# Value products of two key tiles in one block of eight half units, over a ring of sixteen exponential buffers

## The reference

```python
def _expert(x, Wqkv, bqkv, Wo, bo, g1, be1, W1, bf1, W2, bf2, g2, be2):
    q, k, v = jnp.split(x @ Wqkv.T + bqkv, 3, axis=-1)      # each to 8 heads of 16
    attn = jax.nn.softmax(jnp.einsum('bhqd,bhkd->bhqk', q * scale, k), axis=-1)
    ctx = jnp.einsum('bhqk,bhkd->bhqd', attn, v)            # heads joined again
    x = _layernorm(x + ctx @ Wo.T + bo, g1, be1)
    h = jax.nn.gelu(x @ W1.T + bf1, approximate=False)
    h = jax.nn.gelu(h @ W2.T + bf2, approximate=False)
    return _layernorm(x + h, g2, be2)
```

## Time and profile before

| what | us |
|---|---|
| median of the runs | 5361.68 |
| profiled execution, its own time | 5363.5 |
| its span | 5361.7 |
| TensorE busy | 4544.8 (85%) |
| ScalarE busy | 2978.1 (56%) |
| VectorE busy | 2919.5 (54%) |
| granted TensorE clock, mean share | 0.907 |

### The profile page before, as it was taken

The page is one execution under the profiler, slowest core; times in us unless marked ns, Lnnn a source line. Parts: engine busy times, 40 slices in busy tenths (PEclk is TensorE's granted clock), DMA queues, the critical chain, the costliest instruction groups (busy, mean ns, idle before and its releaser), DMA issues.

```text
span 5361.7 us, 86367 instructions
## 1 busy us (share of the span) xinstructions
PE 4544.8 (85%) x25404; PEld 2517.8 (47%) x25404; DVE 2919.5 (54%) x6875; ACT 2978.1 (56%) x6402; POOL 706.2 (13%) x477
## 2 busy tenths in 40 slices
PE   4599997888659999788866999978885699997888
PEld 3344443466434444356643444435663344443566
DVE  5577772234457777224445777722444577762244
ACT  1177775643218777564322877755441287775543
POOL 0212221000022222100001222200000122220000
PEclk8699998999769999899966999989996799998999
DMA  2133320000123332000013323100001333220000
GB/s 90 19 46 46 53 33 15 14 21 18 50 28 44 46 46 33 15 16 18 20 48 36 44 40 50 26 15 20 16 20 46 38 46 44 43 40 1 24 12 23
DMA packets 97883, 174.96 MB, mean 33 GB/s; under 512 B 18848, under 2 KB 75600, under 8 KB 96720
## 3 DMA queue, kind: packets, MB, share of 16 engines
q1 hardware_dynamic: 97488, 170.00, 18.2%
HBM read 94.13 MB, written 1.53 MB: 18 GB/s over the span
## 4 chain that ended last, share of the span: by engine, by line
issue 50%; PE 42%; DVE 3%; POOL 1%; POOLq 1%; DMA 1%; DVEq 1%; ACT 1%; SPq 0%; ACTq 0%
PE ps L767 10%; PE ps L803 10%; PE ps L777 9%; PE ps L837 3%; PE ps L846 3%; PE ps L758 2%; PE ps L864 2%; DVE peaks L1520 1%; POOL rstd L526 1%; DMA k_stack<-parts 1%; PE ps L632 1%; PE ps L827 1%; PE ps L869 1%; DVE xn L1364 1%; PE ps L786 0%
## 5 line engine op out<-in xcount | busy, mean ns | idle before, releaser
L1520 DVE TENSOR_REDUCE peaks<-ps 128x1 f32<-128x748 f32 (+1 forms) x1536 | 1404.2, 934 | 504.7 <-PE ps L777 480.1
L1160 ACT ACTIVATE masked<-ps 128x384 f32<-128x384 f32 (+3 forms) x1536 | 680.5, 485 | 192.3 <-PE ps L767 178.6
L1160 ACT ACTIVATE probs<-ps 128x384 f32<-128x384 f32 (+1 forms) x1536 | 662.3, 484 | 93.3 <-PE ps L767 92.5
L526 POOL TENSOR_TENSOR rstd<-var,minus_half 128x6 f32<-128x6 f32 x104 | 138.5, 1331 | 3429.4 <-DVE var L1360 3429.4
L777 PE MATMUL ps<-k_stack,q_stack 96*128 96x374 bf16 (+1 forms) x1536 | 405.6, 349 | 111.9 <-DMA k_stack<-parts 87.4
L767 PE MATMUL ps<-q_stack,k_stack 98*128 98x384 bf16 (+3 forms) x1536 | 451.7, 330 | 0.6
L767 PE MATMUL ps<-shared 98*128 98x384 bf16 (+3 forms) x1536 | 440.1, 327 | 14.1 <-ACT probs L1160 6.8
L1421 DVE TENSOR_REDUCE top<-ps 128x1 f32<-128x128 f32 (+4 forms) x240 | 151.7, 632 | 452.4 <-PEq L696 354.0
L777 PE MATMUL ps<-shared 96*128 96x374 bf16 (+1 forms) x1536 | 372.1, 323 | 4.8 <-DVE peaks L1520 4.0
L1109 ACT ACTIVATE probs<-ps,neg_top 128x128 f32<-128x128 f32 (+4 forms) x240 | 153.2, 641 | 371.9 <-DVE neg_top L1429 318.2
L767 PEld LDWEIGHTS ps<-shared 98*128 98x128 bf16 (+1 forms) x1536 | 145.5, 103 | 353.5 <-ACT masked L1160 141.7
(11 more groups left out here) (269 smaller groups left out, 7984.7 us busy)
## 6 DMA issues: line engine op xcount, KB each, us to landing
shared<-parts SPq DMA_DIRECT2D x192, 187.0 KB, 9.2
wr<-in_l SPq DMA_DIRECT2D x32, 580.5 KB, 3.6
q_stack<-parts SPq DMA_DIRECT2D x96, 187.0 KB, 8.2
k_stack<-parts SPq DMA_DIRECT2D x96, 187.0 KB, 10.4
wts<-in_l SPq DMA_DIRECT2D x32, 514.5 KB, 3.5
shared<-in_tv SPq DMA_DIRECT2D x4, 4096.0 KB, 12.8
wrow<-in_l_rows SPq DMA_DIRECT2D x32, 320.0 KB, 3.9
wts<-in_l SPq DMA_DIRECT2D x32, 257.5 KB, 2.6
```

Of the source, the lines that this page charges most:

```text
L526: pool.tensor_tensor(rstd[:, :], var[:, :], minus_half[:, :], ALU.pow).then_inc(S["rstd_ready"], 1)
L1160: act.activation(probs_ring(u)[0:m, 0:hi - lo], src[0:m, 0:hi - lo], ACT.Exp, scale=float(HD) ** -0.5).then_inc(S["ring_done"], 1)
L1520: v.tensor_reduce(peaks[0:m, g, j, head:head + 1], src[0:m, :, 0:T // 2], XY, ALU.max)\
```

## The change

Blocks 2k and 2k+1 now stand at the same place, behind the score of unit 4(2k+1)+6: the even block moves back by four units, the odd one stays. Eight value products follow each other without anything between. Since block 2k's exponentials are read four units later, the ring of exponentials has sixteen buffers in place of eight. The new ones are memory that the experts don't use otherwise: `probsT`, `merged`, `QT[:, 1, :]`, `V`. The PSUM banks stay as they are: three for the ring, two pairs, one for the value products. Lines behind the first edit move by up to three: 803 becomes 806, 767 becomes 770, 777 becomes 780, 1160 becomes 1163.

```diff
     def weigh(x, b):
 
-        u = SIDE * b + AT["weigh"]
+
+        u = SIDE * (b | 1) + AT["weigh"]
         if (u < UNITS) == (x == e):
             put(u % UNITS, ("weigh", x, b))
             if b % NT == NT - 1:
@@
         def probs_ring(u):
 
-            slot = u % (2 * SIDE)
-            return (probs, masked)[slot // 4][:, slot // 2 % 2, slot % 2 * H0:(slot % 2 + 1) * H0]
+            slot = u % (4 * SIDE)
+            buf = (probs[:, 0, :], probs[:, 1, :], masked[:, 0, :], masked[:, 1, :], flat(probsT), merged[:, 0:TP],
+                   QT[:, 1, :], flat(V)[:, 0:TP])[slot // 2]
+            return buf[:, slot % 2 * H0:(slot % 2 + 1) * H0]
```

## The result

The changed kernel takes 5463.32 us (median of 4 runs, 5461.86 to 5465.31), the kernel before 5361.43 us on the same chip (5360.40 to 5362.54). The ratio is 1.019, 95% interval 1.0173 to 1.0208: 102 us slower. The forecast was 5466. The profiled execution took 5461.89 us, with a span of 5460.1.

A forecast was written before the change was run, and what follows sets the result against it. TensorE was taken to bound the experts, ACT and DVE barely keeping up. Per usual expert 2.24 us saved and 5.8 more waiting made +3.55, +105 over all: profiled 5468.5, less 1.8, 5466 us; range 5405 to 5515.

The forecast's parts named there:

- What a join saves: On TensorE, one way out of and into a block: 0.187 us per block saved, 2.24 an expert, 72 in all.
- 0.05 shorter: Unknown step at the join, taken as a 0.35 us pass: if 0.05 us shorter, the sum is +87 us.
- two dearer cases: Step at the join costing 0.09 us more: +137 us; costing way out and way in: about +170 us.
- What is paid in waits: TensorE waiting for ACT and DVE in a usual expert: 5.8 us more, so +3.55 us after the saving.
- ACT and the ring of three banks: Units 42 to 50: score 50 waits for the fifth exponential; period 4.01 us, before 3.88, 0.13 more.
- DVE and the two pairs: Units 66 to 74: peaks 72 and 74 wait for their pairs; period 4.59 us, before 4.37, 0.22 more.
- The output product: Units 10 to 18: peaks 16 and 18 wait for pairs; period 6.35 us, before 5.72, 0.63 more.
- The attention turned at unit 8: First period, from unit 2: the turning waits for a division that is lifted later, +0.27 us.
- The period from 82: Eleventh of an expert's twelve periods, eight scores from unit 82: a change of -0.04 us.
- Edits at no cost: New buffers, ACT's and DVE's order, DMAs and the SP and POOL queues: nothing added; the later lift is covered.
- What would show it: Usual expert about 77.6 us, TensorE busy below 72, blocks 1.4 to 1.5, ACT idle about 1.2 at each.
- that the saving stays: Rival in the experts: ACT and DVE catch up and 72 us are gained, 5290 us; chance 0.10.

The follow-up runs named there:

- experiment 1: The kernel before with only the sixteen exponential buffers of the change, value products still in blocks of four at their old places: 5362.81 us, ratio 1.0002.
- experiment 9: The changed kernel with exponentials of 64 columns in experts 1 to 7 and peak reductions over 32 of 374 columns per half: 5255.82 us, ratio 0.9801.
- experiment 2: The changed kernel with the even block one score ahead of the odd one, so the two are not joined: 5506.08 us, ratio 1.027.

## Why the prediction was right

The median lies 3 us from the forecast. By its steps:

- **What a join saves** was too small. The forecast had 0.187 us for way out and way in, with a pass of 0.35 us at the join. The blocks of the changed kernel (medians over the trace, 384 columns) go 0.256 in, 0.347, 0.323 and 0.323 between passes, 0.438 out. The second and third distance are 0.024 shorter than the first, which is the only one that a block of two passes has. So a join saves 0.187 + 2 x 0.024 = 0.235 us, 2.82 us for an expert and 90 for the kernel, not 72. The bound "0.05 shorter" held it. The prediction took the pass as the nearest row for the join, but one lay nearer: before the change, 28 blocks of 364 columns are followed not by a score but by the shift rows (L786, 8 output columns), and those start 0.306 us behind the last pass where a score takes 0.422, the very distance of the later passes in a joined block. Its two dearer cases are a little low: 0.09 and 0.187 us more at each of 384 joins are 35 and 72 us, which would make +140 and +177 where it has +137 and about +170.
- **What is paid in waits** was too small by nearly as much. A usual expert grew by 3.38 us in the trace, so its waits grew by 3.38 + 2.82 = 6.2 us, not 5.8. The two errors (0.58 and 0.4 us) nearly cancel: +3.38 was measured and +3.55 forecast. Single periods were off by up to 0.3 us in both directions, and so were the other experts: expert 0 has +1.10 (forecast 1.6), expert 6 +4.36 (3.2), expert 7 +3.28 (3.6). That the median came within 3 us is thus luck in part; that the kernel would lose some 100 us is not.
- **ACT and the ring of three banks:** right. The wait after a block of 1.15 us stands in the row at 529.83, and the period from 42 is 4.09 us, forecast 4.01. Score 50 comes 2.49 us behind the first score of the period and not 2.34, since a peak stands right before it, which the bare sum left out; way in and block take 1.60 and not 1.67. Short exponentials took the whole growth of this period away and turned it to -0.10. The Trainium skill, "TensorEngine Tiling (Array Packing)", section PSUM Bottleneck, warns that tiling does not speed up the emptying of PSUM. The trace agrees in so far as the joined block gives ACT nothing for 1.15 us in the row at 529.83, and the scores behind it then go at ACT's pitch, 0.37 us apart.
- **DVE and the two pairs:** right in its place, almost to the hundredth. Forecast 1.68, 2.53 and 2.85 us behind the first score for peaks 72 and 74 and score 74, measured 1.69, 2.53 and 2.86. Short peaks took the growth of this period away, short exponentials did not. DVE has fewer periods than was taken before the cuts were run (a distance of 60 us was expected with short peaks, and 81 measured): from 74, the growth went with short exponentials (+0.06), not with short peaks (+0.45).
- **The output product:** right, +0.63 us. Peaks 16 and 18 were forecast 1.09 us apart and start at 495.71 and 496.81.
- **The attention turned at unit 8:** the right wait, at half its size, +0.52 instead of +0.27. Its chain had lost the block that covered it, and it's a cost that neither the exponentials' nor the reductions' length lowers. The last period is its like at the other end, where a score waits for the keys. So is the fifth (from 34), forecast +0.66 and measured +0.60: the prediction named the ten peaks between the feed-forward products, but 0.58 us of waiting stands behind them, at peak 40, for DVE's addition of the way back, and some 0.25 more at the last peak of the period, which short peaks take away.
- **The period from 82** was the largest miss, -0.36 where -0.04 was forecast. The trace of before shows where it comes from. The earlier trace rows is in this period: a peak waited there for DVE, which had just come from its merge:

```profile
540.42 1.34 DVE L1503 COPY gcol<-gates 128x6 f32<-128x6 f32 x1
...
541.83 1.14 DVE L1560 SCALAR_TENSOR_TENSOR h<-y,gcol,h 128x128 f32<-128x128 f32 x4
```

From score 85 to score 86 it was 1.09 us (mean of experts 1 to 5), and 0.48 with short peaks, so 0.6 us of waiting; after the change it is 0.54, for the doubled block stands ahead of that peak and DVE has caught up. Against that, about 0.46 us more went on the shift rows, which wait for ACT's ring. The period was also unsteady before (5.18 to 5.59 us), and so is the copy: in expert 3 it took 1.34 us and ended 0.03 us after an instruction of POOL that ran when it began (539.92 to 541.73), while in expert 2, where none ran, it took 0.16. No run took the copy or the merge away.
- **Edits at no cost:** right for the buffers (experiment 1) and for the rest of the program, which is 3.7 us shorter in the traces, nearly all of it scatter.
- **What would show it:** the length of an expert, the places of the waits that were named and the block's length came as said; the waits at peak 40 and at the keys had not been named. Two signs were wrong. TensorE's busy time did not fall under 72 us but rose to 74.19, because short waits are drawn as busy. And ACT idles about 1.2 us at some blocks only; over the twelve of expert 3 it is 0.43 to 1.2, and 0.57 in the dense stretch, since ACT was behind when the block began.

How the 102 us divide, by the cuts: the distance is 102 whole, 49 without ACT's part, 81 without DVE's, 17 without both. The part of ACT's exponentials is thus 53 to 65 us and that of DVE's reductions 20 to 33, depending on which is cut first and give or take the scatter of the runs. With both cuts the joins still save their 90 us and the order still loses by 17, so some 107 us of waiting stay when exponentials are halved and reductions quartered. The largest of these waits are the four seen in the traces of experiment 9: two for chains through the turning and the keys, two for a pair that DVE's addition still reads. No run took any of them away.

The rivals: that the saving stays, or that both cancel, fails by the result. That the join saves little fails by experiment 2 and by the block's own rows. The clock stood at 0.97, 1.00 and 1.00 in the windows of experts 0, 3 and 7, the same as before. The fall that the Trainium skill, "TensorE: Matmul & The Clock Gate", section "A second HAM failure mode: psum-queue depth-cycling", tells of did not appear here, with TensorE idle for 3.3 of 77.5 us in expert 3.

## What to carry to other kernels

Before blocks on the producer are merged to save a switch, add up the period through the consumer. Here that is the block with its way in, the consumer's start behind the first new piece, its pitch for each piece until the bank of the last one is free: 0.25 + 1.42 + 0.36 + 4 x 0.365 + 0.52 = 4.01 us, where TensorE alone needs 3.54 (the period from 42 with short exponentials). Scores wait where the first sum is the longer, and the merge loses where it also exceeds the period before, 3.88 here. That three banks of 0.365 us don't cover 1.7 us without a score says only that the consumer runs dry, and this alone does not decide: exponentials of 0.22 us are covered still less, and with them the wait was gone, because ACT caught up in time. So a consumer that is 79% busy on average may have no slack: after the gap it catches up at its own pitch, and the producer pays for what is left of that. Look also for chains of other engines that the moved block used to cover: here such waits are 0.4 to 0.9 us each, no smaller than those for the two consumers. In the one run that moved a step of such a chain, the wait only moved with it.

## What the runs showed that was not expected

- Passes of the value products in one block follow each other more closely after the first two: 0.347 us and then 0.323, 0.323 for 384 columns, 0.330 and then 0.306, 0.306 for 364. The forecast used the first distance for all.
- DVE's idle time (480 to 573 us) and TensorE's waits for DVE (115 to 145 us) grew together, with the same work on DVE.
- Shorter work on either consumer speeds up the kernel before, in which TensorE was 99% busy in an expert: 42 us with ACT's exponentials halved. With DVE's reductions cut to a quarter it is 78 us, but of these the experts hold only some 21 (4.9 to 5.6 us in each batch); most lies ahead of them, where the first group's peaks stand without exponentials (the first expert starts at 254.89 us instead of 269.86). Both orders have that part nearly alike (15.0 us ahead of the first expert before, 14.1 after), so it hardly touches the distances above.
